# A three-layer graph convolution: 28 dense tiles in the first layer, a reordered start, one-hots by fours

## The chip, the cores and the metric

The kernel runs on one core of a Trainium2 chip. The metric is the device time of one execution in microseconds (us). Engines are named as in the profile: PE (TensorE), DVE (VectorE), ACT (ScalarE), POOL (GpSimd) and SP (SyncE, which here only issues DMAs).

## The reference

6250 nodes with 256 features; 200,000 edges from `src` to `dst`, sorted by `dst`, with destinations drawn as the square of a uniform number, so low nodes have many edges and high ones few.

```python
x = x + gnn(layernorm(x))            # three layers, each:
#   h = x @ W;  agg[d] = sum over edges (s, d) and the loop (d, d) of h[s] * dinv[s] * dinv[d];  agg + b
#   relu after the first and the second layer; dinv = rsqrt(degree)
x = x + ffn(layernorm(x))            # router x @ wr; of all nodes the 3124 with the highest score:
#   y = gelu(sel @ w1 + b1) @ w2 + b2, times the score, added at their rows
```

## The kernel before, in words

The nodes lie in 49 tiles of 128. A layer's sum over edges is done per tile of destinations, in one of two ways. A **dense** tile multiplies a 128 x 6272 piece of the adjacency matrix (counts, f16) with the features: 49 matmuls of 512 columns (high and low f16 half of 256 features side by side). A **gathered** tile takes its edges in steps of 128: POOL fetches 128 feature rows by an indirect DMA (`fetch_row`, L1371), DVE makes a one-hot of their destinations (`spot_step`, L727), PE multiplies both (L922). `DENSE = (32, 32, 34)` says how many tiles are dense in each layer; 34 pieces of adjacency are built once.

**Units.** `merged(layer)` writes one list of PE's work per layer: dense units (one matmul of 49) with gathered units spread between them. All engines walk through the same list: each has tables of what it does at unit u (`SUM_AT`, `TURN_AT`, `PROD_AT`, `SPOTS`, `STORES`, `LOOPS_AT`, `FETCH_AT`), and each does its part strictly in order.

**Building.** The adjacency is built in the first layer. Edges in 2022 steps, two of them a *pair* j (1011 pairs): `one_hots(j)` on DVE makes a low one-hot for four steps at once (L684) and a wide high one-hot per step (L688); `step(s)` on PE multiplies the two (L884); `evac_group` on ACT copies the sums out of PSUM (L1136, L1140), eight groups per tile, into one of three ring slots; POOL adds the self loops (`add_loops`, L1377); SP stores the piece, 1568 KB (`store_tile`, L1453). A slot is used again when its tile's dense units are done and its store has landed. `due_units()` says how many units PE may have done after pair j (`DUE`): a tile's dense units come directly behind its building. Pairs 0 to 139 (`SCAN`) build tile 0 and have no units beside them, but everything else the start still owes: statistics of x on ACT, the first product per tile (`product_first`, L870; `BEFORE = 12` of them ahead of the pairs and one at each of the pairs 0 to 36), unpacking the edges (`unpack`, `turn_batch`, `settle`), counting degrees (`digits`, `from_row`, `hot_tiles`), scaling the features (`low_first`, L693).

**The start.** Each window of destinations has to be found in the sorted list. POOL fetches ten rows of it (L1287), DVE counts in them (L559), PE spreads the results over the steps (L1006: 28 small f32 products, in the profile 56 records), DVE turns them into addresses (L567 to L569), and POOL fetches the edges (L1297): 3 chunks first (`FIRST_CHUNKS`), then 16. Only then `unpack(0)` and the first pair.

**Behind a tile.** When all units of tile q are done, DVE sums it (L710, L712), PE turns it (L928), ACT applies relu (L1154), PE multiplies with the next weights (L936), ACT and DVE split the result (L1160, L717), SP stores the rows. `spill(l)` on POOL, PE and ACT handles edges beyond the planned steps; it runs at least one round, a chain of indirect DMAs.

After the third layer comes `finish`: selection of the nodes and the feed-forward part.

Of the kernel before, what the change touches and what calls it, by code (L numbers as in the profile page):

```python
# [8 lines left out]
ALU = mybir.AluOpType  # L9
# [7 lines left out]
P = 128  # L17
# [13 lines left out]
DENSE = (32, 32, 34)  # L31
# [41 lines left out]
IDLE_WINDOWS = ((TILE_WINDOW[GATHERED] if TWICE else DWIN, DWIN), (SPARSE0, SPARSE0 + TWICE))  # L73
# [23 lines left out]
BATCH_AT = [0] + [6 * b for b in range(1, len(BATCHES))]  # L97
FIRST_CHUNKS = 3

# [43 lines left out]
SPARSE_TO = [n * TILES - 30 for n in DENSE]  # L143
# [7 lines left out]
def merged(layer):  # L151
    dense = [(t, i) for t in range(DENSE[layer]) for i in range(TILES)]
    sparse = []
    for t in range(DENSE[layer], TILES):
        sparse += [(t, i) for i in range(1 + steps_gathered(t))] + [None] * PAUSE[layer]
    sparse, n, out = sparse[:-PAUSE[layer]], 0, []
    for d, u in enumerate(dense):
        out.append(u)
# [3 lines left out]
    return out  # L162


SEQUENCES = [merged(l) for l in range(3)]
# [30 lines left out]
EASE = 24  # L196


def units_until(n):
    x = n if n <= EASE or not TWICE else EASE + (n - EASE) * (DENSE[0] - 1 - EASE) / (DENSE[0] - EASE)  # L200
    x = min(x, DENSE[0] - 1 + (0.3 if n > DENSE[0] else 0))
    t = int(x)
    whole = END[DENSE_Q[t - 1]] if t else 0
    return whole + int((x - t) * (END[DENSE_Q[t]] - whole))
# [22 lines left out]
BOUND_AT = (2, 7, 12, 17)  # L227
SPILL_FIRST_AT = 46
DIGITS_AT = BATCH_AT[-1] + 6
# [6 lines left out]
DINV_AT = DEGREES_AT + 4  # L236
LOW_AT = DINV_AT + 3
# [5 lines left out]
            for m in range(len(FETCHED))]  # L243

# [14 lines left out]
SPOTS = by_unit([u - 60 for u in STEP_UNIT])  # L259
# [3 lines left out]
def bank_table():  # L263
    banks, before, last, d = [], [], {}, 0
    for q in sorted(range(len(Q)), key=START.__getitem__):
        if not IS_DENSE[q]:
            b = 2
# [18 lines left out]
LOOPS_AT = [START[DENSE_Q[n]] if n < DENSE[0] else DUE[TILE_PAIR[n + 1] - 1] for n in range(TD)]  # L286
STORES = by_unit([DUE[TILE_PAIR[n + 1] - 1] for n in range(TD)])
# [32 lines left out]
def graph(nc, ctx, space, gathered_in, ones, route, small, smalli, b1_sb, br_b, x, x_turned, dst_rows, dst_over, dst_last, edges, gw, gb, wr, br, b1, b2, pair_dram):  # L320
# [12 lines left out]
    tab_dram = dram("tab_dram", (WNS, 4))  # L333
# [45 lines left out]
    def items_of(l):  # L379
# [3 lines left out]
    hots_area = sb("hots", [P, HOTS, P], F16)  # L383
    hots_f = hots_area[:].rearrange("p s n -> p (s n)").bitcast(F32)
# [28 lines left out]
    key_s, src_s = sb("key_s", [P, CHS * P]), sb("src_s", [P, CHS * P], I32)  # L413
# [18 lines left out]
    table = sb("table", [P, WCOLS, 4])  # L432
# [26 lines left out]
        "degrees_back", "degrees_ready", "rooted"))  # L459
    (hot, used, evac, looped, stored_0, stored_s) = (sem(n) for n in (  # L460
# [26 lines left out]
    nexts, worst_row = pw[1][:, 0, 64:64 + WCOLS], pw[1][:, 0, 128:256]  # L487
# [6 lines left out]
    extra_degrees = ag[1][:, 400:401]  # L494
# [6 lines left out]
    with nc.Block() as block:  # L501
        @block.vector
        def _(dve):
# [29 lines left out]
            done(dve.tensor_copy(tile_i[:], counted[:]), "tile of each window")  # L533
            dve.wait_ge(p_sum, 1)
            for f in range(HALVES):
                noted(dve.scalar_tensor_tensor(gw_sb[:, 0, f], colsum, -1.0 / D, gw_sb[:, 0, f], ALU.mult, ALU.add), "centred")
            dve.wait_ge(p_const, 2)
            done(dve.tensor_copy(first_col, consts_2), "first steps")
            dve.wait_ge(c_pool, CONSTANTS)
            for k, a, b in PICKS:  # L540
                q, at_s = QUOTA[a], PICK_AT[k] + FIRST[a] - FIRST[k * P]
                noted(dve.tensor_scalar(pick[:, at_s:at_s + q * (b - a)].rearrange("p (w i) -> p w i", i=q),
                                        which_row[:, a:b].unsqueeze(2).broadcast_to([P, b - a, q]), which_col[:, k:k + 1], None,
                                        ALU.is_equal), "picks")
            dve.wait_ge(p_const, 3)
            done(dve.tensor_tensor(spans_of[:, 1:3], next_consts, cols[:, 1:3, 0:WCOLS], ALU.subtract))
            noted(dve.tensor_copy(step_cols[:, :, 0], thr_col))
            done(dve.tensor_copy(step_cols[:, :, 1], width_col))
            dve.wait_ge(over_in, 16)
            done(dve.scalar_tensor_tensor(area_t[:, 0:ET], over[:, 0:ET], 1.0, over[:, 1:ET + 1], ALU.mult, ALU.is_gt,  # L550
                                          accum_out=order), "order")
            dve.wait_ge(c_pool, CONSTANTS + LATER_CONSTANTS)
            done(dve.tensor_copy(iota_many[:], iota16[:, 0:P].unsqueeze(2).broadcast_to([P, P, 4])))
            dve.wait_ge(p_order, 1)
            done(dve.tensor_copy(ordered[:, 1:2], disorder))
            done(dve.tensor_scalar(ordered[:, 0:1], ordered[:, 1:2], 0.0, None, ALU.is_equal))
            for k in range(WCOLS):
                dve.wait_ge(row_in[k], 16)
                noted(dve.tensor_scalar(lesser[1][:, k * P:k * P + P], found_rows[:, k], thr_col[:, k:k + 1], 0.0, ALU.is_lt,  # L559
# [1252 lines left out]
```

## Time and profile before

| | us |
|---|---|
| median of 3 runs | 2503.58 |
| lowest and highest | 2496.18 and 2523.75 |
| the profiled execution, its own time | 2526.53 |
| its span, first to last instruction | 2524.8 |
| PE busy | 1990.7 (79%) |
| DVE busy | 1200.9 (48%) |
| POOL busy | 1061.4 (42%) |
| ACT busy | 526.2 (21%) |
| mean granted clock of PE | 0.885 |

The span divides into: start and scan up to the first tile (0 to 236 us), building of 33 more tiles beside the first layer (236 to 1104), the end of that layer (to 1121), second layer (to 1777), third layer (to 2255), selection and feed-forward (to 2525). "Busy" is the share in which an engine had an instruction running; DMA issues of SP do not count. A granted clock of 1.00 is 2.4 GHz, 0.50 is 1.2 GHz. A releaser called "remote" is one that the profile cannot name. Some records of PE are missing.

### The profile page before, as it was taken

Reading aid. Unit: us, or ns where it says so; the run is one execution under the profiler, and the core shown is the slowest. Engines: PE = TensorE matmul, PEld = TensorE weight load, DVE = VectorE, ACT = ScalarE, POOL = GpSimd, SP = SyncE. Lnnn points to the kernel's source line nnn. Section 1 sums busy time; section 2 is a strip of 40 time slices with the busy share of each in tenths; the row PEclk is TensorE's granted clock in tenths of the full one; section 3 lists DMA queues with packets and bytes.
Section 4 is the critical chain, followed back from the end, with each engine's and each line's share of the span. In section 5 each row is a group of like instructions: output and inputs, shape, how many; then the busy total and the mean of one; then the engine's idle time right before and its main releaser. Section 6 shows DMA issues by size and latency. Waiting matters only on the chain. (4 is left out here: it accounts for less than half of the span.)

```text
span 2524.8 us, 30366 instructions
## 1 busy us (share of the span) xinstructions
PE 1990.7 (79%) x10096; PEld 1083.4 (43%) x10096; DVE 1200.9 (48%) x4912; ACT 526.2 (21%) x1126; POOL 1061.4 (42%) x1217
## 2 busy tenths in 40 slices
PE   7754587777877878888888888889888878764898
PEld 6542344444443444543433344334333333333566
DVE  5689697667665655642222222220344444454122
ACT  5704132223333333430111111110000000000210
POOL 4300304343353545513465566651466656523111
PEclk8955798888888979988999999989999989885999
DMA  6236523333343434554555556554577767555000
GB/s 232 67 104 213 184 98 121 116 119 122 114 160 118 163 118 160 171 213 172 177 183 179 181 197 203 186 170 149 195 240 239 259 206 247 199 173 158 24 17 24
DMA packets 167007, 402.21 MB, mean 159 GB/s; under 512 B 28651, under 2 KB 118945, under 8 KB 154056
## 3 DMA queue, kind: packets, MB, share of 16 engines
q1 hardware_dynamic: 109976, 255.74, 28.6%
q0 software_dynamic: 50592, 138.13, 17.8%
q10 hardware_dynamic: 6288, 6.42, 0.8%
q8 instruction: 84, 1.38, 0.2%
q14 instruction: 67, 0.55, 0.1%
HBM read 284.18 MB, written 116.01 MB: 159 GB/s over the span
## 5 line engine op out<-in xcount | busy, mean ns | idle before, releaser
L1371 POOL DMA_INDIRECT space_rows<-row_dram,src_s x947 | 908.3, 959 | 599.8 <-PE ag L922 233.2
L911 PE MATMUL ag<-space_a,space_ring 128*128 128x512 f16 x2107 | 659.6, 398 | 11.8 <-POOL space_ring L1377 11.1
L884 PE MATMUL pw<-space_tables 128*128 128x147 f16 (+1 forms) x2022 | 345.7, 257 | 195.1 <-DVE space_tables L688 73.0
L688 DVE TENSOR_SCALAR space_tables<-iota,space_tables 128x148 f16<-128x148 f16 (+1 forms) x2022 | 427.7, 271 | 0.1
L884 PEld LDWEIGHTS pw<-space_tables 128*128 128x128 f16 x2022 | 215.2, 118 | 426.3 <-DVE space_tables L688 126.8
L922 PE MATMUL ag<-space_rows,hots 128*128 128x512 f16 x947 | 371.5, 392 | 13.3 <-DVE hots L727 8.0
L1136 ACT ACTIVATE space_ring<-pw 128x784 f16<-128x784 f32 (+1 forms) x257 | 219.0, 857 | 505.4 <-PE pw L884 330.7
L684 DVE TENSOR_TENSOR space_tables<-iota_many,space_tables 128x512 f16<-128x512 f16 x506 | 212.2, 419 | 168.3 <-remote 92.6
L911 PEld LDWEIGHTS ag<-space_a,space_ring 128*128 128x128 f16 x2107 | 207.7, 102 | 122.9 <-issue 14.6
L911 PE MATMUL pw<-space_b,space_ring 128*128 128x512 f16 x784 | 216.8, 399 | 8.4 <-DVE space_work L712 8.4
L1377 POOL TENSOR_TENSOR space_ring<-space_ring,ident 128x128 f16<-128x128 f16 x34 | 18.2, 534 | 433.0 <-ACT space_ring L1140 254.5
L727 DVE TENSOR_SCALAR hots<-iota,key_s 128x128 f16<-128x128 f16 x947 | 199.4, 266 | 1.6
L911 PE MATMUL pw<-space_a,space_ring 128*128 128x512 f16 x686 | 177.1, 389 | 9.1 <-issue 7.2
L717 DVE SCALAR_TENSOR_TENSOR space_a<-both,per_node,space_a 128x256 f16<-128x256 f32 x49 | 23.7, 484 | 308.5 <-ACT space_a L1160 222.7
L1146 ACT ACTIVATE space_work<-space_work,per_node 128x256 f32<-128x256 f32 x147 | 72.8, 503 | 341.9 <-DMA space_work<-extra 225.1
L936 PE MATMUL both<-gw_sb,space_work 128*128 128x256 f32 x392 | 113.2, 415 | 34.9 <-issue 21.9
L922 PEld LDWEIGHTS ag<-space_rows,hots 128*128 128x128 f16 x947 | 95.6, 101 | 102.5 <-issue 29.4
L1154 ACT ACTIVATE space_work<-both,gb_sb 128x128 f32<-128x128 f32 x196 | 61.2, 364 | 357.5 <-remote 210.6
L911 PEld LDWEIGHTS pw<-space_b,space_ring 128*128 128x128 f16 x784 | 80.1, 102 | 103.3 <-issue 15.7
L928 PE MATMUL both<-ident,space_work 128*128 128x128 f32 x196 | 43.7, 309 | 93.6 <-DVE space_b L717 41.9
L911 PE MATMUL ag<-space_b,space_ring 128*128 128x512 f16 x392 | 110.6, 399 | 0.0
L911 PEld LDWEIGHTS pw<-space_a,space_ring 128*128 128x128 f16 x686 | 68.2, 100 | 96.4 <-issue 19.5
(346 smaller groups left out, 1880.5 us busy)
## 6 DMA issues: line engine op xcount, KB each, us to landing
space_ring<-adj SPq DMA_DIRECT2D x49, 1568.0 KB
adj<-space_ring SPq DMA_DIRECT2D x34, 1568.0 KB
space_tables<-adj SPq DMA_DIRECT2D x17, 1568.0 KB
space_work<-extra SPq DMA_DIRECT2D x147, 128.0 KB
space_rows<-row_dram,src_s POOLq DMA_INDIRECT x947
extra<-hots SPq DMA_DIRECT2D x2, 6272.0 KB, 32.0
space_b<-in_x_turned SPq DMA_DIRECT2D x7, 896.0 KB, 12.6
space_a<-in_x SPq DMA_DIRECT2D x7, 896.0 KB, 6.0
```

The lines of the kernel that those rows point to most:

```text
L684: dve.tensor_tensor(olo[:, r // 2], iota_many[:], slo[:, 2 * j:2 * j + 4].unsqueeze(1).broadcast_to([P, P, 4]), ALU.is_equal)
L688: ins = dve.tensor_scalar(ohi[:, r, i, 0:n], iota16[:, 0:n], key[:, 2 * j + i:2 * j + i + 1], None, ALU.is_equal)
L727: dve.tensor_scalar(hots_area[:, g % HOTS, :], iota16[:, 0:P], key_s[:, s:s + 1], None, ALU.is_equal).then_inc(spot, 1)
L884: pe.matmul(pw[v % 2][:, half, at_c:at_c + n], olo[:, j % RING // 2, :, j % 2 * 2 + i], ohi[:, j % RING, i, 0:n], start=s == FIRST[w], sto ...
L911: mm = pe.matmul(bank(q), a[:, k, :], hh[l][:, k, :], start=i == 0, stop=i == TILES - 1)
L922: pe.matmul(bank(q), hots_area[:, g % HOTS, :], slots[g % GR], start=False, stop=i == n).then_inc(g_used, 1)
L928: mm = pe.transpose(px[:, f * P:(f + 1) * P], u_sb[:, q % 2, f * P:(f + 1) * P], ident[:])
L936: mm = pe.matmul(ph[:, 0:D], fresh[:, q % 2, f, :], gw_sb[:, l, f, :], start=f == 0, stop=f == HALVES - 1)
L1136: act.activation(target[:, :, d:d + n].rearrange("p s (h d) -> p s h d", h=2), pw[v % 2][:, :, 0:n // 2 * TILES].rearrange("p h (d s) -> p ...
L1146: act.activation(ep[:, q % 2], ep[:, q % 2], ACT.Copy, scale=unfactor[:, l, t:t + 1]).then_inc(e_scaled, 1)
L1154: ins = act.activation(fresh[:, q % 2, f, :], px[:, f * P:(f + 1) * P], ACT.Relu, bias=gb_sb[:, l, f:f + 1])
L1371: pool.indirect_dma_start(slots[g % GR], None, row_dram[STEP_LAYER[g]], bass.IndirectOffsetOnAxis(src_s[:, s:s + 1], 0)).then_inc(g_in[g % ...
```

## The change

1. `DENSE` goes from (32, 32, 34) to (28, 32, 34). The first layer has 28 dense and 21 gathered tiles, the others stay. All 34 pieces are still built, as the third layer uses them; tiles 28 to 33 are built and stored without dense units of the first layer.
2. `FILL`: behind the last dense tile 112 empty places are put into the first layer's list, and gathered units are spread over these too; `units_until` is written anew, so that the 28 dense tiles are through about one tile after their building, and the rest of the list lies beside the last building.
3. The start: `order` and its product come ahead of `centred`; only window column 0 is worked off (`lows(slice(0, 1))`, `picks(True)`), then the first 3 chunks' products, their addresses and their edge fetches; the other nine columns, the other 17 chunks' products and fetches and `step_masks` lie in the scan, at the pairs 6, 8 to 24, and 25. Ahead of the pairs there are 4 first products rather than 12, then one at every other pair up to 89. 20 statistics operations on ACT are ahead of the pairs rather than 32, then four per three pairs rather than three per pair. POOL fetches 6 window rows, the first edges, then 4 window rows. Tables, quotas, the spill of degrees and so on move to later pairs.
4. Tile 1's self loops (`PE_LOOPS = 1`) are a matmul of PE with the identity, ahead of its units; POOL adds them to the stored piece only after tile 2's, and the piece is stored after its units.
5. The one-hots of gathered steps are made by fours (`spot_steps`), one tensor_tensor of 128 x 512 for four tensor_scalar of 128 x 128; `key_s` becomes f16, the ring of one-hots six groups of four.
6. Gathered tiles of the first layer may use PSUM banks 0 and 1 once no dense tile needs them. The first evacuation waits for the addresses of all chunks rather than for the last unpacking.

```diff
-DENSE = (32, 32, 34)
+DENSE = (28, 32, 34)
...
-BATCH_AT = [0] + [6 * b for b in range(1, len(BATCHES))]
+BATCH_AT = [0, 6] + [32 + 4 * b for b in range(len(BATCHES) - 2)]
...
-SPARSE_TO = [n * TILES - 30 for n in DENSE]
+FILL = (28 * max(TD - DENSE[0] - 2, 0), 0, 0)
+SPARSE_TO = [n * TILES - 30 + f + (20 if f else 0) for n, f in zip(DENSE, FILL)]
...
-    dense = [(t, i) for t in range(DENSE[layer]) for i in range(TILES)]
+    dense = [(t, i) for t in range(DENSE[layer]) for i in range(TILES)] + [None] * FILL[layer]
...
-EASE = 24
+EASE = 16
 def units_until(n):
...
+    end = DENSE[0] + 1
+    if n <= EASE:
+        at = n * TILES
+    elif n <= end:
+        at = EASE * TILES + (n - EASE) * (DENSE[0] - EASE) * TILES // (end - EASE)
+    else:
+        at = DENSE[0] * TILES + (n - end) * FILL[0] // (TD - 1 - end)
+    return UNITS_UPTO[min(at, len(UNITS_UPTO) - 1)]
...
-BEFORE = 12
-PRODUCT_AT = [t - BEFORE for t in range(TILES)]
-STATS_BEFORE = 32
-STATS_EACH = 3
-NEXT_AT, WORST_AT, ROUNDS_AT = 1, 5, 9
-SPILL_FIRST_AT = 46
+AHEAD_OF_STEPS, BEFORE = 2, 4
+PRODUCT_AT = [t - BEFORE if t < BEFORE else 1 + 2 * (t - BEFORE) for t in range(TILES)]
+STATS_BEFORE = 20
+EARLY_ROWS = 6
+REST_AT, STEPS_FROM, STEPS_AT = 6, 8, 25
+NEXT_AT, WORST_AT, ROUNDS_AT = 28, 31, 34
+SPILL_FIRST_AT = 82
...
-LOOPS_AT = [START[DENSE_Q[n]] if n < DENSE[0] else DUE[TILE_PAIR[n + 1] - 1] for n in range(TD)]
-STORES = by_unit([DUE[TILE_PAIR[n + 1] - 1] for n in range(TD)])
+LOOPS_AT = [START[DENSE_Q[n]] if n < DENSE[0] else DUE[TILE_PAIR[n + 1] - 1] + 44 for n in range(TD)]
+STORES = by_unit([END[PE_LOOPS] + 4 if n == PE_LOOPS else DUE[TILE_PAIR[n + 1] - 1] for n in range(TD)])
...
+            picks(True)
+            dve.wait_ge(p_const, 3)
...
+            lows(slice(0, 1))
+            dve.wait_ge(c_pool, CONSTANTS + LATER_CONSTANTS)
+            place_steps(0)
+            done(dve.tensor_copy(iota_many[:], ...))
+            picks(False)
...
-                dve.tensor_scalar(hots_area[:, g % HOTS, :], iota16[:, 0:P], key_s[:, s:s + 1], None,
+                dve.tensor_tensor(hots_area[:, n % (HOTS // 4)], iota_many[:], key_s[:, s:s + 4].unsqueeze(1).broadcast_to([P, P, 4]),
...
+                    own = l == 0 and t == PE_LOOPS
+                    if own and i == 0:
+                        pe.matmul(bank(q), ident16[:], hh[l][:, t, :], start=True, stop=False)
...
+            pe.wait_ge(c_dve, steps["low of step zero 0"])
+            for c in range(FIRST_CHUNKS):
+                chunk_steps(c)
+            for t in range(AHEAD_OF_STEPS, BEFORE):
+                product_first(t)
...
+            fetch_window_rows(range(EARLY_ROWS))
+            fetch_edges(0)
+            fetch_window_rows(range(EARLY_ROWS, WCOLS))
...
+            add_loops(PE_LOOPS + 1)
+            add_loops(PE_LOOPS)
+            n_looped = PE_LOOPS + 2
```

## Rows read from the trace of the kernel before

**Rows 1.** Busy time by stretches: us, five engines (instructions), PE clock, DMA share, GB/s
```profile
56.00:90.00 34.00, 24.82 (x116) 18.62 (x115) 22.96 (x97) 23.59 (x99) 22.84 (x30) 0.88 0.42 113
...
190.00:236.00 46.00, 17.04 (x83) 6.14 (x84) 41.38 (x157) 23.35 (x54) 0.00 (x0) 0.50 0.51 169
236.00:283.00 47.00, 29.73 (x193) 14.35 (x191) 39.64 (x195) 7.16 (x10) 11.50 (x22) 0.86 0.84 289
...
582.00:999.00 417.00, 320.07 (x1804) 184.22 (x1802) 251.46 (x1131) 138.61 (x228) 190.84 (x205) 0.87 0.41 137
999.00:1104.00 105.00, 92.28 (x533) 53.64 (x531) 69.86 (x304) 49.36 (x81) 47.22 (x52) 0.97 0.50 170
...
1190.00:1777.00 587.00, 491.87 (x2135) 236.66 (x2133) 123.72 (x473) 72.63 (x194) 315.76 (x343) 0.92 0.53 178
```

**Rows 2.** Timeline (start, us, what, [idle, releaser]): loops of tiles 11, 27, 29, 33
```profile
581.66 0.48 POOL L1377 TENSOR_TENSOR space_ring<-space_ring,ident 128x128 f16<-128x128 f16 x1 [14.35 <-ACT space_ring L1136]
...
999.13 0.68 POOL L1377 TENSOR_TENSOR space_ring<-space_ring,ident 128x128 f16<-128x128 f16 x1 [0.22 <-ACT space_ring L1136]
...
1041.51 0.44 POOL L1377 TENSOR_TENSOR space_ring<-space_ring,ident 128x128 f16<-128x128 f16 x1
...
1103.88 0.43 POOL L1377 TENSOR_TENSOR space_ring<-space_ring,ident 128x128 f16<-128x128 f16 x1 [9.09 <-ACT space_ring L1136]
```

**Rows 3.** Timeline of one halt behind a tile's store, around 610 us
```profile
605.73 0.32 SPq L1453 DMA_DIRECT2D adj<-space_ring  x1
...
624.58 0.35 PE L884 MATMUL pw<-space_tables 128*128 128x196 f16 x1 [10.08 <-ACT space_ring L1136]
```

**Rows 4.** Groups, DVE and POOL, 582-999 us: busy, mean ns, idle before, releasers
```profile
L688 DVE TENSOR_SCALAR space_tables<-iota,space_tables 128x148 f16<-128x148 f16 (+2 forms) x699 | 150.0, 272 | 0.0
L684 DVE TENSOR_TENSOR space_tables<-iota_many,space_tables 128x512 f16<-128x512 f16 x174 | 73.1, 420 | 88.2 <-remote 60.5 <-PE pw L884 27.1 <-issue 0.2
L727 DVE TENSOR_SCALAR hots<-iota,key_s 128x128 f16<-128x128 f16 x182 | 46.6, 256 | 0.0
...
L712 DVE SCALAR_TENSOR_TENSOR space_work<-ag,per_node,space_work 128x256 f32<-128x256 f32 x25 | 12.1, 484 | 0.9
...
L1371 POOL DMA_INDIRECT space_rows<-row_dram,src_s x189 | 182.7, 967 | 83.5 <-issue 45.3 <-PE ag L922 23.1 <-remote 13.8
L1377 POOL TENSOR_TENSOR space_ring<-space_ring,ident 128x128 f16<-128x128 f16 x16 | 8.5, 529 | 156.9 <-ACT space_ring L1140 106.6 <-ACT space_ring L1136 50.3
```

**Rows 5.** Timeline of the start, POOL, PE and DVE
```profile
21.46 1.18 POOL L1287 DMA_INDIRECT space_rows<-in_dst_rows,tile_i  x1 [12.87 <-DVE cols L538]
...
40.56 12.11 PE L1006 MATMUL ag<-step_cols,space_ring 128*128 128x3 f32 x56 [5.46 <-DVE step_cols L564]
42.75 0.98 POOL L1297 DMA_INDIRECT space_ring<-in_edges,step_i  x1 [6.63 <-DVE step_base L569]
...
55.88 0.42 DVE L684 TENSOR_TENSOR space_tables<-iota_many,space_tables 128x512 f16<-128x512 f16 x1 [1.33 <-ACT space_tables L1121]
```

**Rows 6.** Groups of instructions on DVE and PE in the scan, 56 to 236 us
```profile
L684 DVE TENSOR_TENSOR space_tables<-iota_many,space_tables 128x512 f16<-128x512 f16 x72 | 30.3, 421 | 16.5 <-PE pw L884 14.9 <-ACT space_tables L1121 1.3
L870 PE MATMUL both<-gw_sb,space_b 128*128 128x256 f32 x75 | 22.1, 420 | 8.8 <-ACT space_b L1108 8.8
```

**Rows 7.** Timeline of PE: a product, start of the second layer, 49 dense units
```profile
1105.45 1.03 PE L936 MATMUL both<-gw_sb,space_work 128*128 128x256 f32 x4
...
1120.26 5.27 PE L911 MATMUL pw<-space_b,space_tables 128*128 128x512 f16 x12 [6.01 <-DMA space_tables<-adj]
...
1797.19 10.75 PE L911 MATMUL pw<-space_a,space_ring 128*128 128x512 f16 x49 [1.77 <-DVE space_b L712]
```

**Rows 8.** Timeline around tile 1, all engines
```profile
236.14 0.42 POOL L1377 TENSOR_TENSOR space_ring<-space_ring,ident 128x128 f16<-128x128 f16 x1 [99.56 <-ACT space_ring L1140]
...
270.16 0.25 ACT L1140 ACTIVATE space_ring<-pw 128x98 f16<-128x98 f32 x1
...
283.51 0.61 PE L911 MATMUL ag<-space_a,space_ring 128*128 128x512 f16 x1 [11.13 <-POOL space_ring L1377]
```

More of the change, by code:

```diff
@@ L161, in merged @@
             n += 1
-    return out
-SEQUENCES = [merged(l) for l in range(3)]
+        upto.append(len(out))
+    return out, upto
+SEQUENCES = [merged(l)[0] for l in range(3)]
+UNITS_UPTO = merged(0)[1]
 ORDERS = [sorted(range(TILES), key=lambda t: max(n for n, u in enumerate(s) if u[0] == t)) for s in SEQUENCES]
@@ L533, in _ @@
             done(dve.tensor_copy(tile_i[:], counted[:]), "tile of each window")
+            dve.wait_ge(p_const, 2)
+            done(dve.tensor_copy(first_col, consts_2), "first steps")
+            dve.wait_ge(over_in, 16)
+            done(dve.scalar_tensor_tensor(area_t[:, 0:ET], over[:, 0:ET], 1.0, over[:, 1:ET + 1], ALU.mult, ALU.is_gt,
+                                          accum_out=order), "order")
             dve.wait_ge(p_sum, 1)
@@ L545, in _ @@
[L545 to L559, printed above, removed]
-                                        ALU.add, accum_out=inside[:, k:k + 1]))
@@ L561, in _, with picks @@
-            dve.wait_ge(c_dve, steps["all"])
-            done(dve.scalar_tensor_tensor(low, counted[:], float(P), inside[:], ALU.mult, ALU.add))
-            done(dve.tensor_scalar(low, low, ordered[:, 0:1], None, ALU.mult), "low")
-            done(dve.scalar_tensor_tensor(step_cols[:, :, 2], first_col, float(-P), low, ALU.mult, ALU.add), "low of step zero")
-            for i, c in enumerate((slice(0, FIRST_CHUNKS), slice(FIRST_CHUNKS, CH))):
+            def picks(first):
+                for k, a, b in PICKS:
+                    if (k == 0) == first:
+                        q, at_s = QUOTA[a], PICK_AT[k] + FIRST[a] - FIRST[k * P]
+                        noted(dve.tensor_scalar(pick[:, at_s:at_s + q * (b - a)].rearrange("p (w i) -> p w i", i=q),
+                                                which_row[:, a:b].unsqueeze(2).broadcast_to([P, b - a, q]), which_col[:, k:k + 1],
+                                                None, ALU.is_equal), "picks")
@@ new lines, in lows @@
+            def lows(ks):
+                for k in range(ks.start, ks.stop):
+                    dve.wait_ge(row_in[k], 16)
+                    noted(dve.tensor_scalar(found_rows[:, k], found_rows[:, k], thr_col[:, k:k + 1], 0.0, ALU.is_lt,
+                                            ALU.add, accum_out=inside[:, k:k + 1]))
+                dve.wait_ge(c_dve, steps["all"])
+                done(dve.scalar_tensor_tensor(low[:, ks], counted[:, ks], float(P), inside[:, ks], ALU.mult, ALU.add))
+                done(dve.tensor_scalar(low[:, ks], low[:, ks], ordered[:, 0:1], None, ALU.mult), "low")
+                done(dve.scalar_tensor_tensor(step_cols[:, ks, 2], first_col[:, ks], float(-P), low[:, ks], ALU.mult, ALU.add),
+                     f"low of step zero {ks.start}")
@@ L993, in _ @@
                       skip_group_check=True).then_inc(p_const, 1)
-            for t in range(BEFORE):
+            pe.wait_ge(c_dve, steps["order"])
+            pe.matmul(disorder, ones[:], order, start=True, stop=True, skip_group_check=True).then_inc(p_order, 1)
+            for t in range(AHEAD_OF_STEPS):
                 if t == 0:
@@ L1283, in _ @@
             pool.wait_ge(c_init, 4)
-            pool.wait_ge(c_dve, steps["tile of each window"])
-            for k in range(WCOLS):
-                pool.indirect_dma_start(found_rows[:, k, :], None, dst_rows,
-                                        bass.IndirectOffsetOnAxis(tile_i[:, k:k + 1], 0)).then_inc(row_in[k], 16)
             pool.iota(iota16[:], pattern=[[1, WC]], base=0, channel_multiplier=0, **small_ok).then_inc(c_pool, 1)
```

169 lines of the change are left out of this document (103 added, 66 removed).

## The prediction

> **What bounds the kernel now.** I read the stretches first [rows 1]. Up to 236 us DVE is the busiest engine, never full: 22.96 of 34 us, later 41.38 of 46. While tiles are built beside the first layer (582 to 999) PE is busy 320 of 417 us, DVE 251, POOL 191, ACT 139. Tile 11's loops are added at 581.66, tile 27's at 999.13 [rows 2]: 26.1 us per tile, 20 of them PE. The other 6 are halts: 9 us after a tile's store is issued PE halts for 10.08 us, released by an evacuation of ACT [rows 3]. In 582 to 999 DVE sat 60.5 us before L684 for "remote" releasers [rows 4]; I don't know what these are, but they come with stores, and the change keeps all 34. Between halts PE sets the pace, so in this stretch a unit more costs its time. In the second layer PE is busy 492 of 587 us and DVE 124 [rows 1]: PE-bound, and its list is not changed.
>
> **The profiled execution** took 2526.53 us, span 2524.8. The median of the three runs is 2503.58, so 23 lower. I sum against the profile and carry the difference over to the median.
>
> **The start: -17, with the scan -25.** The first pair begins at 55.88 [rows 5]. On its way stand the counting in ten rows, all 28 products (12.11 us from 40.56), and PE's 12 first products ahead of them. After the change: POOL starts its first row fetch at 21.46; the last of six is done at about 30 (six by some 1.25, one slow); `edges` follows. DVE and PE, free from 21 too, have `order`, 15 picks, one row and 3 products (12.11 / 28 = 0.43 each) to do, by my estimate 8 us. Edges go out at 31 instead of 42.75 and are landed, unpacked, turned and settled some 7 us later. ACT has 20 statistics ahead of that rather than 32. First pair at 38 to 39: 17 earlier. Owed later: nine rows, addresses and masks, 4 us of DVE, a third table column 0.7, and 25 products, 11 us of PE.
>
> The scan then: pairs 0 to 36 now carry a first product each, PE is the later engine there, and DVE waits 14.9 us for PE before L684 [rows 6] besides waits for column sums. Spread over 90 pairs, a product (4 records, 1.03 us in the like of it at L936 [rows 7]) stands beside two pairs rather than one. A column takes 0.219 / 512 us [rows 7], so the four steps of 147 columns add 0.25: PE has 1.3 us for two pairs, DVE 1.0 (twice the 0.50 of tile 1, below) plus its share of unpacking. That takes some 12 of the waits away; at the pairs 8 to 24 the moved products give 4 back. Nothing behind pair 100 changes but for offsets. So 17 + 12 - 4 (waits) - 5 (owed on DVE) = 20 by the lower, and with ACT's idle time also filled up to 33. I take 25. Ends: 8 (waits only move) and 35.
>
> **Tile 1's loops: -11.** Tile 1 is evacuated at 270.16, but POOL is in `spill(0)` and adds its loops only at 283, and PE stands 11.13 us [rows 8]. With the identity on PE (0.22 us) that halt is gone. What is late next: tile 2's loops need POOL out of the spill; tile 2 takes 48 pairs by 0.50 (34.0 us from 236.14 to 270.16 for 68 pairs) from 270, so 294, later than 283. The store of piece 1 moves behind tile 2's; its slot is wanted by tile 4, two tiles on. Ends: -7 and -16.
>
> **One-hots by fours.** A single costs 256 ns (L727), a group what L684 costs, 420 ns on the same 512 elements and the same broadcast [rows 4]. In the first layer 420 / 4 x 0.42 = 44 us rather than 330 x 0.256 = 84; in the others 617 x 0.256 = 158 becomes 65. DVE is not the bound there, so most of it is covered by PE. It also issues some 690 instructions fewer between halts. I take -5, ends 0 and -20; a loss is possible only where a group waits for its fourth step's slot: six groups, issued 60 units ahead, leave 40 units.
>
> Here a rule speaks against the change. POOL's instructions, nearly all fetches, take 190.84 / 205 = 0.93 us busy each at 582 to 999, where DVE works 251 of 417 us, a third of it in this form (L684), and 315.76 / 343 = 0.92 at 1190 to 1777, where DVE is at 124 of 587 and never uses it [rows 1]. The Trainium skill ("SBUF — State Buffer", Who interferes with whom) says that a DVE instruction with two SBUF inputs contends with POOL's reads, which the four-step form is and the single was not. By the rule POOL's fetches would lengthen; by the rows by 1% at most. It enters the POOL rival below and not the sum.
>
> **First layer, to tile 29: +22.** I worked out the lists from the code. At the end of tile 29's pairs PE has been let through 1686 units before and 1765 after: 79 more, and 45 products rather than 41. A dense unit is 10.75 / 49 = 0.219 us, a product with its turn 1.1 [rows 7], both at clock 1.00 or near; the clock here is 0.87 [rows 1]: (79 x 0.215 + 4 x 1.1) / 0.87 = 24.6. Some falls into PE's waits for DVE: 22. Ends: 8 (halts absorb it) and 35.
>
> **Tiles 30 to 33: -12.** From 1041.51 to 1103.88 they take 62.4 us [rows 2] beside 185 units. After it is 46 units; 64 pairs are then DVE's: 64 by 0.50 as in tile 1 and 0.03 more for the wider one-hots, my estimate, 34; five sums of three operations by 0.484 [rows 4], 7; nine groups by 0.42, 4; one short halt, 5: 50 us. Ends: 42 (tile 1's pace, 0.50 per pair, no halt) and 58.
>
> **The seam: +3.** The second layer's first piece is fetched after the last pair, into space that the pairs use. Its first unit starts at 1120.26, 16.4 us after tile 33's loops, and PE stood 6.01 of these [rows 7]; 44 units lay in it. After it is 2. So the 44 units (9 us), taken from behind the pairs, give nothing: the fetch is the path. PE then starts cold: the clock was 0.50 at 190 to 236, where it worked 17 of 46 us [rows 1], so the first units cost double, +3 (0 to +6).
>
> **Second layer on:** lists, fetches and banks are the same: 0, plus or minus 5.
>
> Sum: -25 - 11 - 5 + 22 - 12 + 3 = **-28**: the profile would be 2498, the median **2476**.
>
> **Rivals.**
> (1) The start's gain does not carry. For: DVE had waits before and has 5 us more to do; PE gets the moved products. Then the start gives 8 to 10 rather than 25: 2491. Chance 0.25.
> (2) POOL becomes the bound of the building, ending slower. It has 384 fetches rather than 291 up to tile 29, 3.7 more per tile, 16 in all. One costs 0.967 + 45.3 / 189 = 1.21 us, so 19.5, and 0.53 for the loops. It now also waits 156.9 / 16 = 9.8 us per tile for the last evacuation, fetches queued behind [rows 4]. That wait must shrink below 27 - 20 = 7 us; it decides at that point. If all of it stays, a tile takes 29.8 rather than 27: 25 tiles by 2.8 = +70: 2546. Against: the wait comes from being early, and up to 16 rows are fetched ahead. Chance 0.15.
> (3) The last tiles run at the lower clock. While PE waits for DVE in every pair with no units beside, the clock is 0.50 (190 to 236), with units 0.86 (236 to 283) [rows 1]. At 0.50 a column takes twice 0.219 / 512 us, so PE needs 128 steps x 0.168 + 46 units x 0.438 + 4 products x 2.2 = 50 us there, no cover for a halt, +10: 2486. Chance 0.1. The Trainium skill ("TensorE: Matmul & The Clock Gate", Loop structure matters more than you think) puts it on the loop nest whether matmuls stay warm; the rows agree.
> (4) Fewer DVE instructions and shifted stores shorten the 6 us of halts per tile by a quarter, 27 tiles x 1.5 = 40: 2436. Chance 0.05.
>
> **Numbers.** Forecast 0.45, rivals 0.25, 0.15, 0.1, 0.05. Range 2442 to 2518: all but the far end of (2), and the open ends of start, middle and tail. A measurement tells about 1% (25 us) from no change. Faster by more: 0.50. Within: 0.34, as rivals 1 and 3 and the forecast's weak end lie there. Slower: 0.16.
>
> **What would show it.** First L684 at 38 to 39; tile 0's loops at 207 to 218 rather than 236.14; no halt of PE before tile 1's units; tiles 11 to 27 at 27 to 28 us each; PE's wait for gathered rows near none; tiles 30 to 33 in 50 us; 16 to 17 us from tile 33's loops to the second layer; that layer as long as now. The prediction is wrong if tile 0 is not 15 us earlier, if POOL's wait for evacuations falls to zero while PE waits for rows, or if the second layer's length changes by over 10 us.

## The result, and the profile after

The median before is 2511.7 us and after 2547.7, ratio **1.0144** (95% 1.0075 to 1.0212): slower by some 1.4%, where 2476 was forecast. The profiled runs took 2526.53 and 2545.01 us, spans 2524.8 and 2543.3. That of before lies 15 above its median, so the profiles show 18.5 of the 36.

The stretches of after, with the columns of [rows 1]: the end of the scan, the pairs of tiles 1 and 2, tiles 5 to 29, the last tiles, and the second layer.

```profile
190.00:224.50 34.50, 12.68 (x62) 4.63 (x62) 31.02 (x117) 16.12 (x37) 0.00 (x0) 0.50 0.58 193
224.50:286.00 61.50, 52.13 (x336) 24.94 (x334) 61.50 (x295) 13.69 (x17) 12.77 (x23) 0.97 0.68 232
368.00:1074.00 706.00, 519.41 (x2917) 301.95 (x2916) 404.24 (x1666) 214.95 (x359) 381.86 (x403) 0.88 0.44 141
1089.00:1115.00 26.00, 17.19 (x97) 10.25 (x97) 20.14 (x88) 16.16 (x23) 10.59 (x12) 0.80 0.68 246
1130.00:1798.00 668.00, 554.00 (x2393) 269.31 (x2393) 113.74 (x242) 76.88 (x203) 338.60 (x375) 0.91 0.53 178
```

The timeline of after at the points of [rows 2, 5, 7, 8]: first one-hot, loops of tiles 0, 2 and 1, 11, 27, 29 and 33, then the first matmuls of the second layer and of its end.

```profile
37.38 0.43 DVE L716 TENSOR_TENSOR space_tables<-iota_many,space_tables 128x512 f16<-128x512 f16 x1 [1.08 <-ACT space_tables L1178]
...
224.51 0.42 POOL L1450 TENSOR_TENSOR space_ring<-space_ring,ident 128x128 f16<-128x128 f16 x1 [51.97 <-ACT space_ring L1200]
...
285.90 1.11 POOL L1450 TENSOR_TENSOR space_ring<-space_ring,ident 128x128 f16<-128x128 f16 x2 [13.62 <-ACT space_ring L1196]
...
586.95 0.80 POOL L1450 TENSOR_TENSOR space_ring<-space_ring,ident 128x128 f16<-128x128 f16 x1 [9.05 <-ACT space_ring L1196]
...
1032.43 0.44 POOL L1450 TENSOR_TENSOR space_ring<-space_ring,ident 128x128 f16<-128x128 f16 x1
...
1074.39 0.44 POOL L1450 TENSOR_TENSOR space_ring<-space_ring,ident 128x128 f16<-128x128 f16 x1
...
1115.21 0.43 POOL L1450 TENSOR_TENSOR space_ring<-space_ring,ident 128x128 f16<-128x128 f16 x1 [6.46 <-ACT space_ring L1196]
...
1130.00 0.61 PE L952 MATMUL pw<-space_b,space_tables 128*128 128x512 f16 x1 [14.21 <-DMA space_tables<-adj]
...
1797.97 0.58 PE L993 MATMUL pw<-space_tables 128*128 128x512 f16 x1 [8.85 <-POOLq L1390]
```

Against before, the first pair is 18.5 us earlier, tile 0's loops 11.6, tile 3's 25.1 (320.36, before 345.47). Then it turns: tile 11's are 5.3 us later, tile 29's 32.9. The last four tiles take 40.8 us instead of 62.4, and tile 33 is 11.3 late. The second layer grows by 11.2, the rest shrinks by 2.5. So 58 us are lost between tiles 3 and 29.

What PE and POOL did in tiles 5 to 29 (groups, columns of [rows 4]), after:

```profile
L964 PE MATMUL ag<-space_rows,hots 128*128 128x512 f16 x369 | 146.6, 397 | 5.4 <-DMA space_rows<-row_dram,src_s 4.2 <-issue 1.0
L920 PE MATMUL pw<-space_tables 128*128 128x196 f16 x681 | 123.3, 263 | 67.2 <-ACT space_ring L1196 34.7 <-issue 27.7 <-DVE space_tables L720 4.9
L920 PE MATMUL pw<-space_tables 128*128 128x147 f16 x462 | 73.6, 239 | 40.2 <-ACT space_ring L1196 29.3 <-issue 10.9
L970 PE MATMUL both<-ident,space_work 128*128 128x128 f32 x82 | 18.7, 315 | 63.7 <-DVE space_b L749 41.6 <-issue 22.1
L1450 POOL TENSOR_TENSOR space_ring<-space_ring,ident 128x128 f16<-128x128 f16 x24 | 11.8, 493 | 155.9 <-ACT space_ring L1196 109.3 <-ACT space_ring L1200 46.5
```

and before (391 to 1041 us):

```profile
L922 PE MATMUL ag<-space_rows,hots 128*128 128x512 f16 x281 | 110.5, 393 | 0.0
L884 PE MATMUL pw<-space_tables 128*128 128x196 f16 x681 | 122.8, 261 | 69.4 <-ACT space_ring L1136 50.0 <-issue 14.2 <-DVE space_tables L688 5.0
L884 PE MATMUL pw<-space_tables 128*128 128x147 f16 x462 | 73.9, 240 | 43.3 <-issue 32.5 <-ACT space_ring L1136 10.5 <-DVE hots L727 0.3
L928 PE MATMUL both<-ident,space_work 128*128 128x128 f32 x76 | 17.0, 311 | 40.0 <-DVE space_b L717 40.0
```

With the small groups counted in, PE stood 187 us in after and 153 before, and hardly ever for rows. It was busy 519.4 us, before 496.8: this new work was foreseen, the 34 us more of standing were not.

**What a halt looks like.** After's timeline around 530 us, POOL, ACT, DVE and PE:

```profile
512.21 0.45 POOL L1450 TENSOR_TENSOR space_ring<-space_ring,ident 128x128 f16<-128x128 f16 x1 [12.01 <-ACT space_ring L1196]
512.81 0.97 POOL L1442 DMA_INDIRECT space_rows<-row_dram,src_s  x1 [0.15 <-issue]
514.08 1.10 POOL L1442 DMA_INDIRECT space_rows<-row_dram,src_s  x1 [0.30 <-issue]
...
533.21 0.95 POOL L1442 DMA_INDIRECT space_rows<-row_dram,src_s  x1 [0.30 <-issue]
...
524.95 0.82 ACT L1196 ACTIVATE space_ring<-pw 128x784 f16<-128x784 f32 x1 [7.27 <-PE pw L920]
536.97 0.47 ACT L1220 ACTIVATE space_b<-both,per_node 128x256 f16<-128x256 f32 x1 [11.20 <-remote]
...
527.82 0.43 DVE L716 TENSOR_TENSOR space_tables<-iota_many,space_tables 128x512 f16<-128x512 f16 x1 [3.64 <-remote]
...
537.48 0.48 DVE L749 SCALAR_TENSOR_TENSOR space_b<-both,per_node,space_b 128x256 f16<-128x256 f32 x1 [8.85 <-ACT space_b L1220]
...
523.48 1.02 PE L978 MATMUL both<-gw_sb,space_work 128*128 128x256 f32 x4
...
538.10 0.66 PE L970 MATMUL both<-ident,space_work 128*128 128x128 f32 x2 [13.38 <-DVE space_b L749]
```

POOL was held 12 us for an evacuation, then issued 17 fetches one behind another, 512.8 to 534.2. ACT's L1220 waits for nothing but PE's product (L978), whose record ends at 524.5; it ran at 536.97, after the burst, and DVE and PE stood behind it. In tiles 5 to 29 of before there are 19 halts of PE over 3 us, 126 us in all, and all but one (6 fetches) overlap a **burst** of 7 or more, most of them beginning 7 to 10 us into it. These bursts cover only 0.38 of that time. One of the halts is that of [rows 3]: its store at 605.73 is followed by 15 fetches, 605.86 to 624.5. After has 17 halts there, 120 us, all of them at such bursts, which cover 0.56 of the time. It has 23 bursts of 8 or more instead of 15, and 66 us of waits under 3 us instead of 27. Not every burst halts PE: each of the 15 long ones of before holds a halt over 3 us, but only 13 of the 23 of after.

**Which engine is late.** It is PE. The trace also has the times at which semaphores were raised (the counters by which an engine tells the others that something is done). The product's was raised at 536.94, 12.4 us after the end of its record, and ACT began 0.03 us later; so ACT did not stand with its wait met. PE's semaphore of L920 was raised at 524.92, 525.66, 527.77, 527.80, 530.61, 535.51 and 535.54, where no matmul is on record, and DVE's L716 ran at 527.82 behind one of these. The profile models the ends of matmuls, so a matmul's record doesn't tell when its result was there. In the building (tiles 5 to 29) 11 of 37 products of before and 15 of 38 of after had their semaphore raised over 3 us after the record's end, up to 17.0, while of some 1800 times of DVE's and ACT's semaphores in both kernels all but one lie within 0.15 us of the end of an instruction. This also settles the "remote" of [rows 4]: all of the 60.5 us before L684 end with PE's semaphore of L884, raised over 1.5 us after the end of the last L884 matmul on record, so that the profile names nobody.

Theory H, formed here: the bursts hold PE up, and DVE and ACT stand behind it, and 28 tiles lengthen them. Rivals: the store (S), the bytes of the fetches (D), the gathered units as such (U), one of the joined changes (B).

### The profile page after: what moved, and what is told of

Its sections match the earlier page's. It is cut to its first block and busy times, and to the rows that moved or that the text cites. A ratio compares the mean times of both kernels' runs of the same rounds, so it can differ in the third digit from the quotient of the medians.

```text
span 2543.3 us, 29665 instructions
## 1 busy us (share of the span) xinstructions
PE 1977.6 (78%) x9999; PEld 1079.8 (42%) x9999; DVE 1144.3 (45%) x4232; ACT 526.9 (21%) x1126; POOL 1160.6 (46%) x1309
## 5 line engine op out<-in xcount | busy, mean ns | idle before, releaser
L1442 POOL DMA_INDIRECT space_rows<-row_dram,src_s x1037 | 1006.6, 971 | 649.8 <-PE ag L964 276.3
L952 PE MATMUL ag<-space_a,space_ring 128*128 128x512 f16 x1911 | 606.8, 397 | 3.2 <-issue 3.1
L920 PE MATMUL pw<-space_tables 128*128 128x147 f16 (+1 forms) x2022 | 345.3, 257 | 195.7 <-ACT space_ring L1196 74.0
L720 DVE TENSOR_SCALAR space_tables<-iota,space_tables 128x148 f16<-128x148 f16 (+1 forms) x2022 | 421.5, 271 | 0.0
L964 PE MATMUL ag<-space_rows,hots 128*128 128x512 f16 x1037 | 409.4, 395 | 15.1 <-DVE hots L759 7.6
L920 PEld LDWEIGHTS pw<-space_tables 128*128 128x128 f16 x2022 | 212.8, 119 | 431.4 <-DVE space_tables L720 119.9
L716 DVE TENSOR_TENSOR space_tables<-iota_many,space_tables 128x512 f16<-128x512 f16 x506 | 211.7, 418 | 130.6 <-PE pw L920 70.1
L952 PEld LDWEIGHTS ag<-space_a,space_ring 128*128 128x128 f16 x1911 | 188.4, 102 | 100.7 <-issue 15.5
L964 PEld LDWEIGHTS ag<-space_rows,hots 128*128 128x128 f16 x1037 | 119.9, 116 | 106.0 <-issue 23.9
L978 PE MATMUL both<-gw_sb,space_work 128*128 128x256 f32 x392 | 105.9, 394 | 28.5 <-issue 15.9
L759 DVE TENSOR_TENSOR hots<-iota_many,key_s 128x512 f16<-128x512 f16 x260 | 114.7, 456 | 10.0 <-PE ag L964 7.3
L742 DVE SCALAR_TENSOR_TENSOR space_work<-ag,per_node,space_work 128x256 f32<-128x256 f32 x78 | 37.4, 480 | 161.9 <-remote 94.3
```

The lines of the kernel that those rows point to most:

```text
L716: dve.tensor_tensor(olo[:, r // 2], iota_many[:], slo[:, 2 * j:2 * j + 4].unsqueeze(1).broadcast_to([P, P, 4]), ALU.is_equal)
L720: ins = dve.tensor_scalar(ohi[:, r, i, 0:n], iota16[:, 0:n], key[:, 2 * j + i:2 * j + i + 1], None, ALU.is_equal)
L759: dve.tensor_tensor(hots_area[:, n % (HOTS // 4)], iota_many[:], key_s[:, s:s + 4].unsqueeze(1).broadcast_to([P, P, 4]), ALU.is_equal).the ...
L920: pe.matmul(pw[v % 2][:, half, at_c:at_c + n], olo[:, j % RING // 2, :, j % 2 * 2 + i], ohi[:, j % RING, i, 0:n], start=s == FIRST[w], sto ...
L952: mm = pe.matmul(bank(q), a[:, k, :], hh[l][:, k, :], start=i == 0 and not own, stop=i == TILES - 1)
L964: pe.matmul(bank(q), hots_area[:, hot_at, :, g - SPOT_GROUPS[SPOT_GROUP_OF[g]][0]], slots[g % GR], start=False, stop=i == n).then_inc(g_us ...
```

## The experiments

Ratios are to the kernel before on the same chip. Stretch runs in this table from the last evacuation of tile 5 to that of tile 29, which all kernels have; the rows shown as windows (391 to 1041, 368 to 1074, 365 to 960) end with POOL's loops of tile 29, 3 to 10 us later. Halts are PE's idle times over 3 us in the stretch, with their sum; "long" counts bursts of 8 or more fetches with under 0.6 us between.

| kernel | ratio (95%) | span | stretch | halts | long |
|---|---|---|---|---|---|
| before | 1 | 2524.8 | 647 | 18, 123 | 15 |
| after | 1.014 (1.008 to 1.021) | 2543.3 | 699 | 16, 117 | 23 |
| e1, 32 tiles | 0.980 (0.978 to 0.982) | 2433.7 | 586 | 15, 82 | 15 |
| e4, start, 32 tiles | 0.987 (0.985 to 0.989) | 2476.9 | 596 | 14, 84 | 13 |
| e8, loops later, 28 | 0.992 (0.989 to 0.995) | 2505.5 | 650 | 14, 65 | 15 |
| e9, own tiles, 28 | 0.994 (0.991 to 0.998) | 2485.4 | 642 | 16, 72 | 12 |
| e10, own tiles, 32 | 0.948 (0.942 to 0.955) | 2380.9 | 525 | 2, 7 | 0 |
| e11, loops later, 32 | 0.959 (0.952 to 0.966) | 2406.5 | 549 | 7, 29 | 7 |
| e14, pause, 28 | 0.973 (0.969 to 0.977) | 2437.6 | 610 | 9, 36 | 0 |
| e15, loops earlier, 32 | 0.991 (0.987 to 0.994) | 2475.1 | 625 | 19, 98 | 20 |
| e16, own tiles, 34 | 0.941 (0.936 to 0.945) | 2347.9 | 476 | 0 | 0 |
| e17, before with pause | 0.949 (0.941 to 0.957) | 2364.1 | 544 | 2, 8 | 0 |
| e18, 34 own, pause | 0.926 (0.919 to 0.933) | 2321.7 | 491 | 3, 12 | 0 |

**Which part of the change costs.** Four kernels, each after with something undone: e1 `DENSE = (32, 32, 34)`, e2 the one-hots one by one, e3 tile 1's loops on POOL, e4 all three of these. e4 keeps the new rule by which units are let through, so it is more than the start.

> The changed kernel with 32 dense tiles in the first layer instead of 28; start, loops of tile 1 on PE and one-hots by fours stay. Theory A (the 28 tiles cost it: 91 more gathered matmuls and four more tile sums while tiles are built, with the stops that go with them, and less given back at the end): 2515, and 25 to 45 below the changed kernel. Rival B (one of the joined changes costs it: the four-step one-hots or the spread start): 2540 to 2550, as the changed kernel. Rival C (the stops after stores fall otherwise in every kernel, whatever is changed): anything between, with PE's idle time of tiles 3 to 29 near 189 us rather than 154.

> The changed kernel with one-hots of gathered steps made one by one (128 columns, 256 ns) rather than four at a time; 28 tiles stay. Theory A: DVE is not the bound, so 2540 to 2560 against the changed kernel's 2548. Rival B (the four-step form costs): 15 us or more below the changed kernel, the second layer about 10 us shorter.

> The changed kernel with tile 1's loops added by POOL after its first spill, as before; 28 tiles stay. Theory A, and my prediction: 7 to 16 us above the changed kernel, 2558. Rival: the halt taken away is paid later (tile 2 or 3), 2545 to 2552.

> Only the start and the spread products are left of the change: 32 tiles, tile 1's loops on POOL, one-hots one by one. Theory A: tile 0's loops at 224 rather than 236 and 8 to 15 us below the kernel before, about 2500. Rival (the start's gain is lost by tile 4 to waits elsewhere): within 5 us of the kernel before.

e1 has a median of 2448.35 us: without the 28 tiles the joined changes gain 2%, and rival B falls. In the profile they take 91 us off, 54 of them in this stretch (595.7 us, before 650.1), where nothing was forecast for them. e4 takes 44 off there too. e1 and e4 share the new start and the new rule of letting units through; which of the two does it was not tried. The tiles alone cost 0.034 of 2500, 85 us (in the profiles 110), twice the 25 to 45 that I expected. By place, from after and e1: the stretch +111, the last four tiles -24, the second layer +20 (668 against 648), the rest +4. Of the 111, PE's busy time is 38 (519.41 against the 481.56 below) and its standing 73 (187 against 113, sums of its groups). e2 came out at 1.022 (1.018 to 1.025), e3 at 1.022 (1.019 to 1.024): each part undone costs at most some 20 us and may cost nothing, as the intervals touch after's. e3's profile shows tile 3's store 12 us later than after's (333.28 against 320.93) and the same span, 2543.5: the gain at tile 1 was taken back later. e4 has a median of 2467.63, far below the 2500 that I expected.

```profile
365.00:960.00 595.00, 481.56 (x2824) 287.53 (x2821) 387.29 (x1625) 209.62 (x345) 297.35 (x313) 0.92 0.44 146
```

This row is e1's stretch, with the same 2824 matmuls as before's.

**Store, slots or burst.** e5 and e6:

```diff
-GR = 16
+GR = 8
-while n_looped < TD and LOOPS_AT[n_looped] <= (STEP_UNIT[g - GR] + 40 ...):
+while n_looped < TD and DUE[TILE_PAIR[n_looped + 1] - 1] + 6 <= STEP_UNIT[g]:
```

e7 stores `adj[n][:, 0:P]` for n of 3 and more, 32 KB rather than 1568; it leaves the rest of these pieces out, and the later layers fetch the first three again and again, so its output is another one, with the same instructions on the engines. e8 has `START[DENSE_Q[n]] + 24` in LOOPS_AT.

> The changed kernel with 8 slots for gathered rows rather than 16, and POOL's loops of tile n placed right behind the pairs of that tile in its list. Theory H (PE's halts in the building are the long bursts in which POOL issues its fetches back to back after it was held for an evacuation; every halt over 3 us in the kernels so far begins 8 to 12 us into a burst of 8 or more and ends with it): bursts of at most 8, at most a quarter of the halts over 3 us left in tiles 5 to 29, 60 us or more shorter than the changed kernel, 2470 to 2490. Rival S (the halts come from the store of the tile, 1568 KB, whatever POOL does): 2540 to 2550. Rival R (8 rows ahead are too few and PE waits for rows): slower, 2560 or more, with PE's wait for gathered rows over 30 us.

> The same with 32 dense tiles in the first layer (against the run with 32 tiles and 16 slots, 2448). Theory H: its bursts are shorter already, so it gains less, 20 to 50: 2400 to 2430. Rival S: 2448. Rival R: 2460 or more.

> The changed kernel with tiles from number 3 on stored by one block of 49 (32 KB rather than 1568 KB); the later layers fetch three stored tiles over and over, so the aggregate is another one. Work on the engines is the same. Theory H: the bursts stay and so do most halts, 2525 to 2545. Rival S: the halts go, 60 us or more shorter, below 2490.

> The changed kernel with POOL's loops of dense tile n placed 24 units later in its list, so that POOL is held less before each tile and has fetched more by then. Theory H: its wait for evacuations falls from 270 us by a third or more, bursts are shorter, 15 to 40 below the changed kernel: 2510 to 2530. Rival S: unchanged. Rival L (PE now waits for the loops at each dense tile): slower by 1 to 3 us per tile, 2575 or more.

e7 came out at 1.012 (1.006 to 1.017), with 18 halts of 121 us from tile 5's loops to tile 29's: **the store has no part in the halts**. e5 is at 1.010 (1.005 to 1.015), e6 at 0.994 (0.991 to 0.996), 1.3% above e1: a miss for H's number, and rival R was right in kind. PE's group of gathered matmuls in e5, 370 to 1050 us:

```profile
L964 PE MATMUL ag<-space_rows,hots 128*128 128x512 f16 x356 | 151.6, 426 | 102.0 <-DMA space_rows<-row_dram,src_s 99.7 <-issue 2.3
```

PE now waits 100 us for rows, while its waits at pairs and turns fall from 171 us to 53. POOL still drains its backlog in bursts, 25 long ones in this window, so this one doesn't test the burst. e8 gives 0.992, 55 us below after by the ratios (expected 15 to 40): POOL's wait for evacuations is 39 us between 370 and 1050, where after has 156 in its stretch.

**Holding POOL less, or more.** In e9 and e10 PE adds the tiles' own rows (`own = l == 0 and 0 < t < OWN`) and POOL adds the loops only when the tile is done. e11 is e1 with `START + 24`, e15 e1 with `START - 16`. e12 has 30 tiles.

> The changed kernel (28 tiles, 16 slots) in which PE adds every dense tile's own rows by one more matmul with the identity (27 by 0.22 us, 6 us), and POOL adds the loops for the later layers only when the tile's units are done, so that it is never held for an evacuation ahead of its fetches. Theory H (long bursts behind POOL's wait are the halts): POOL's wait ahead of loops under 40 us in place of 270, bursts mostly under 8, PE's idle time in tiles 5 to 29 under 120 us in place of 187, 40 us or more below the changed kernel: 2480 to 2510. Rival U (the 28-tile schedule costs PE time by its gathered units as such): within 15 us of the changed kernel.

> The same with 32 dense tiles in the first layer (tiles 1 to 25 by PE, 26 to 31 by POOL, 24 units later in its list). Theory H: 10 to 40 below the run with 32 tiles: ratio to before 0.965 to 0.977. Rival: the bursts of 32 tiles cost little, ratio 0.98.

> 32 dense tiles, loops 24 units later in POOL's list, otherwise the changed kernel. Theory H: 10 to 35 below the 32-tile run, ratio to before 0.967 to 0.976. Rival (PE waits for the loops as much as it saves): 0.98 or more.

> The changed kernel with 30 dense tiles in the first layer. Theory H: between, the price grows with the number of bursts over 8 fetches (18 at 32 tiles, 27 at 28): ratio to before 0.995 to 1.005. Rival (a threshold at 28): 0.98 as with 32.

The place of the loops in POOL's list, nothing else, moves the 32-tile kernel from 0.991 over 0.980 to 0.959, and the long bursts from 20 over 15 to 7. e10 has none and two halts. e10 and e11 both gained more than the ranges that I had given: H had the direction and too small a size. e12 at 0.997 (0.994 to 1.001) lies between 28 and 32: no threshold. e9, at 0.994, lies in my range, but PE still stood 132 us in the stretch where I had set 120, for all that POOL's wait at the loops was 14 us: with 16 fetches per tile POOL issues rows for most of the time, and 12 long bursts and 72 us of halts are left, 5 of the 16 halts not at a burst of 7 or more.

**What in a burst.** e13 gathers rows of half the width (`row_dram[0]` read as twice as many rows of 256), with the same instructions; it leaves out the other half of each row, and its output is another one. e14, after otherwise:

```diff
                 pool.indirect_dma_start(slots[g % GR], None, row_dram[STEP_LAYER[g]], ...)
+                if g < LAYER_STEP[1] and g % 4 == 3:
+                    pool.wait_ge(rested, g // 4)
+                    pool.memset(rest[:, 0:768], 0.0).then_inc(rested, 1)
```

> The changed kernel in which the first layer's gathered steps fetch 512 bytes per row rather than 1 KB (another half row than the layer needs; the matmul reads it twice, so PE's and POOL's instructions are as many and as long, and only the bytes of the fetches are halved). Theory D (the halts are made by the bytes that a burst moves): halts over 3 us of PE in tiles 5 to 29 fall by half, 30 us or more below the changed kernel. Theory Q (made by the back-to-back issue of fetches on POOL, or the number of their descriptors, whatever the bytes): bursts and halts stay, within 15 us of the changed kernel.

> The changed kernel with a memset of 128 x 768 on POOL (some 1.5 us, my estimate from the 128 x 128 one of 0.25 us) behind every fourth fetch of the first layer: POOL is busy all the same, but its fetches are no longer back to back. Theory Q: halts over 3 us become rare (under 6 in tiles 5 to 29), and PE gains 40 us or more less what it then waits for rows; 2490 to 2530. Rival P (any long stretch of POOL at work holds the others, by memory access and not by descriptors): halts stay or grow, 2550 or more.

> 32 dense tiles, POOL's loops of a dense tile 16 units earlier in its list (the later place gave ratio 0.959, the unmoved one 0.980). Theory H: POOL is held longer, bursts of 16 and more are commoner, PE halts more: ratio to before 0.99 to 1.01. Rival: the place of the loops matters only where PE waits for them, ratio 0.98.

> 34 dense tiles in every of the first and third layers (34, 32, 34), tiles 1 to 27 with their own rows added by PE, the rest by POOL 24 units later. Theory H: fewer fetches (some 330 rather than 345 beside the pairs) and bursts under 8, so the building is no slower than with 32 and the last two tiles' 98 units come behind it: within 15 us of the 32-tile kernel with own tiles, ratio 0.945 to 0.955. Rival: the tail behind tile 33 costs all of its units, 20 us: 0.957 or more.

e13 is at 1.019 (1.015 to 1.023), with 21 halts of 122 us from tile 5's loops to tile 29's, while this stretch moves 104 GB/s and not 141: not the bytes. e14 gives **0.973**, some 100 us below after by the ratios (I expected 18 to 58) although POOL has 72 us more to do in the stretch. POOL in e14:

```profile
511.46 1.11 POOL L1443 DMA_INDIRECT space_rows<-row_dram,src_s  x1 [0.30 <-issue]
512.87 1.11 POOL L1443 DMA_INDIRECT space_rows<-row_dram,src_s  x1 [0.31 <-issue]
513.98 0.75 POOL L1447 MEMSET rest<- 128x768 f32 x1
514.90 0.95 POOL L1443 DMA_INDIRECT space_rows<-row_dram,src_s  x1 [0.17 <-issue]
```

For 113 us, 725 to 838, it goes on like this without a rest, 76 fetches, with no halt over 5 us. Work on POOL as such (rival P) is not it. The memset also lowers the mean rate of fetches; whether the rate counts or the number in a row was not separated, nor was a shorter pause tried. e16, at 0.941, is better than the 0.945 to 0.955 that I expected: POOL fetches 236 steps in the stretch rather than e10's 287, and neither a long burst nor a halt is left.

**The pause alone, and the best.** e17 is the kernel before with the same three lines, for all layers. e18 is e16 with them.

> The kernel before with one addition: a memset of 128 x 768 on POOL (0.75 us in the spaced run) behind every fourth gathered fetch, in all three layers. Theory Q: the halts in its building (18 over 3 us between 370 and 1042) and part of the waits of turns and products in the later layers go: 50 to 90 us, ratio 0.965 to 0.98. Rival (the pause helps only where 28 tiles press on POOL): ratio 0.99 to 1.0.

> The 34-tile kernel with own tiles (ratio 0.941), and the same pause behind every fourth fetch in all layers. Theory Q: its first layer has only two halts left, so what is gained lies in the second and third layers, 10 to 30 us: ratio 0.929 to 0.937. Rival (bursts there cost nothing, the pauses only delay rows): 0.941 or more.

e17, groups of PE and POOL in its stretch, 375 to 940 us:

```profile
L885 PE MATMUL pw<-space_tables 128*128 128x196 f16 x723 | 125.8, 255 | 27.3 <-ACT space_ring L1137 10.3 <-issue 9.4 <-DVE space_tables L689 6.2
L885 PE MATMUL pw<-space_tables 128*128 128x147 f16 x462 | 71.5, 234 | 12.6 <-ACT space_ring L1137 7.5 <-issue 4.8 <-DVE hots L728 0.3
L929 PE MATMUL both<-ident,space_work 128*128 128x128 f32 x78 | 16.0, 289 | 25.5 <-DVE space_b L718 16.3 <-issue 9.2
...
L1376 POOL MEMSET rest<- 128x768 f32 x73 | 55.2, 757 | 0.0
L1381 POOL TENSOR_TENSOR space_ring<-space_ring,ident 128x128 f16<-128x128 f16 x25 | 12.0, 479 | 125.3 <-ACT space_ring L1137 77.5 <-ACT space_ring L1141 47.7
```

PE stands 71 us instead of 153 between the loops of tiles 5 and 29 (547.8 us, before 650.1), and 19 halts become two. The second layer begins at 1000.10 (before 1120.26) and takes 626 us (657). There the pause does less for the halts: no burst of 8 is left of 27, but 9 halts of 44 us out of 11 of 55. The median is 2368.35: three lines in the kernel before gain 5.1%, more than expected. e18 is the fastest, **0.926** (0.919 to 0.933), 2317.49 us, a little under the range that I gave.

## Why the prediction was wrong

- **Start, -17: right** (18.5). **With the scan, -25: wrong**, 11.6 by tile 0's loops, under the 15 that I had set as a bound. The scan gave 7 back where I let it gain 8. In one of its waits, which ends at 133.19, PE stands 11.36 us for DVE's one-hots, and POOL issues nothing near it. I didn't try which moved step causes it.
- **Tile 1, -11: right.** Tile 0's to tile 3's loops take 95.9 us, before 109.3, so 13.5 less. The lead of 25 at tile 3 compares with the 36 forecast: the scan lacks 13, and these tiles give 2 more.
- **One-hots, -5:** e2 puts them at 8 to 18 us by medians and ratios, uncertain to some 20.
- **First layer to tile 29, +22: this is the step that failed.** It came to 58 (-25.1 to +32.9). The units were counted rightly, and so was their price: PE's busy time in tiles 5 to 29 grew by 22.6 us over before, where I had 24.6. Not in the sum was the standing, 34 us more than before, and 73 more than e1 with 32 tiles has; against e1 the work is 38 more, at clock 0.88 and not 0.92. I had written that halts "come with stores, and the change keeps all 34". The stores only mark where POOL is let go: the loops release the store on SP and, on POOL, the backlog of fetches. More fetches per tile (16, not 12) make longer bursts, and these cost. "Some falls into PE's waits" was the wrong sign: the units made waits. I also read the "remote" waits of [rows 4] as a sign of stores; they are waits for PE's own late semaphores.
- **Last tiles, -12:** -21.6, 40.8 us, below my lower end of 42. **Seam, +3:** -1.6 (14.8 us from the loops to the first matmul).
- **Second layer, 0 plus or minus 5: wrong**, +11, outside the bound of 10. With the same lists it took 648 us in e1, 649 in e9 and 668 in after: a spread of 20 that I had not allowed for. Fetches come in bursts there too, and e17 ran it 31 us shorter than before; what sets it in a given kernel isn't settled.
- **Rival 2** (POOL becomes the bound, 2546) hit the number by luck and not by its mechanism: PE waited 4.2 us for rows, and POOL still waited 155.9 us for evacuations. That wait, which I read as slack ("comes from being early"), is what piles up the burst. **Rival 4** had the halts as the swing, with the other sign.
- **The four-step form** and POOL: fetches are as long as before, 977 ns against 968, so the contention that I weighed didn't show.

Shown: in the building the halts over 3 us go with the back-to-back fetches, in both directions, for 28, 32 and 34 tiles and in the kernel before, and not with the store, the bytes or POOL's work; and in them PE's semaphores come late, with ACT and DVE behind. Not shown: what a burst takes from PE, whether its matmuls run late or only their semaphores are raised late. Nor is it shown why 10 of 23 long bursts of after pass without a halt, why the second layer keeps its halts under the pause, or what the 9 halts of e14 are, which has no burst over 4.

One rival is late instructions. One of the two instruction queues in the trace moves 84 packets of 16 KB in the run. The Trainium skill ("Runtime: NRT & Kernel Launch", Instruction fetch mechanics) says that each engine's instructions are fetched through a DMA queue in blocks of 16 KB, and calls this mostly hidden. The trace speaks for it at most weakly: 26 of these packets come in after's stretch, one every 27 us or so, and two of them stand within 2 us behind the end of a halt (436.8, halt until 435.87; 466.0, until 464.93). That is about what chance gives for 17 halts, and at those that end at 538.10 and 569.27 there is none. No run here tests it.

## What to carry to other kernels

Where several engines stop together and the releaser is "remote" or "issue", look at what POOL issued in the 10 us before: here 8 or more indirect DMAs in a row stood beside most such halts. Look also at when the semaphore that ends the wait was raised, since the end of a matmul's record doesn't tell it. Break such a row up (a 0.75 us memset behind every fourth took 135 us off), and don't hold the queue that issues them for something that it could do later. An engine's wait is not slack if what piles up behind it is let go at once; and look at halts one by one before giving them a cause, since in the kernel before a store went out 6 to 19 us ahead of every one of them and had no part.

## What was not expected of the hardware

- PE, with DVE and ACT behind it, stands 3 to 13 us in most rows of 8 to 19 indirect DMAs of 128 rows that POOL issues back to back (1.25 us each): in 15 of 15 in before's stretch, in 13 of 23 in after's. The DMA share was 0.36 in the halt shown (524 to 534 us). With a memset of 757 ns in every fourth gap, two of before's 19 such halts are left there.
- In these halts PE's own semaphores are raised up to 17.0 us after the recorded end of the matmul, those of DVE and ACT within 0.15 us.
- Halving the bytes of each such DMA, and cutting the 1568 KB store to 32 KB, left the time within 0.5% of the changed kernel's by the ratios.
- Where the halts are fewer, PE's clock is higher: the mean over its two levels, 1.2 and 2.4 GHz, was 0.88 in the stretch of after (17 halts), 0.92 in e1's (15, but 82 us rather than 120) and 0.99 in e16's, 365 to 880 us (none).
